# Macaron block (FFN, attention, FFN) on one core: another order of norm, unpacking and gelus at the head of both FFNs

## The reference, cut to what matters

```python
x = x + 0.5 * ffn(layernorm(x))            # "FFN 1"
x = x + attention(layernorm(x))            # 16 heads of 32, causal
x = x + 0.5 * ffn(layernorm(x))            # "FFN 2", the same weights

def layernorm(x, eps=1e-5):
    return (x - mean(x)) / sqrt(var(x) + eps)

def ffn(xt):                               # xt: 2048 x 512, MLP 4096
    gate = xt @ dequant(gate_W).T          # 4096 x 512
    up   = xt @ dequant(up_W).T            # 4096 x 512
    gelu = tanh(0.79788 * (gate + 0.044715 * gate**3)) * gate * 0.5 + gate * 0.5
    return (gelu * up) @ dequant(down_W).T # 512 x 4096
```

## Time and profile before

| | us |
|---|---|
| median of 3 runs | 3058.48 (3055.43 to 3061.62) |
| the profiled execution's own time | 3058.05 |
| its span (first to last instruction) | 3056.3 |
| PE busy in the span | 2944.6 (96%) |
| DVE, ACT, POOL busy | 1878.1, 1060.1, 758.6 |
| mean granted clock of PE, share of full speed | 0.982 |

### The profile page before, as it was taken

The page is one execution under the profiler, slowest core; times in us unless marked ns, Lnnn a source line. Parts: engine busy times, 40 slices in busy tenths (PEclk is TensorE's granted clock), DMA queues, the critical chain, the costliest instruction groups (busy, mean ns, idle before and its releaser), DMA issues. The chain is left out here.

```text
span 3056.3 us, 38836 instructions
## 1 busy us (share of the span) xinstructions
PE 2944.6 (96%) x13152; PEld 2208.8 (72%) x13152; DVE 1878.1 (61%) x3314; ACT 1060.1 (35%) x1797; POOL 758.6 (25%) x481
## 2 busy tenths in 40 slices
PE   5999999999999989999999999689999999999999
PEld 3788888888888858754454555368888888888887
DVE  7666565566565555566666665876556656556654
ACT  4322222222222222265565665243222222222222
POOL 4322222222222234400000002343222222222221
PEclk8999999999999989999999999799999999999999
DMA  3000000000000016822322331101000000000001
GB/s 96 21 28 22 27 27 21 21 27 24 24 27 21 1 45 130 220 54 52 62 55 52 62 78 64 45 14 33 23 21 27 21 27 27 21 21 27 21 14 55
DMA packets 120234, 126.75 MB, mean 41 GB/s; under 512 B 72728, under 2 KB 72984, under 8 KB 116820
## 3 DMA queue, kind: packets, MB, share of 16 engines
q1 hardware_dynamic: 120148, 125.71, 15.8%
HBM read 96.34 MB, written 29.34 MB: 41 GB/s over the span
## 5 line engine op out<-in xcount | busy, mean ns | idle before, releaser
L61 PE MATMUL psum<-ffn_x_high,ffn_w_high 128*128 128x512 f32 x2048 | 803.3, 392 | 18.6 <-DVE ffn_gelu L389 18.6
L62 PE MATMUL psum<-ffn_x_low,ffn_w_high 128*128 128x512 f32 x2048 | 799.2, 390 | 0.0
L63 PE MATMUL psum<-ffn_x_high,ffn_w_low 128*128 128x512 f32 x2048 | 798.9, 390 | 0.0
L526 POOL TENSOR_TENSOR ffn_inner<-ffn_gelu,ffn_inner 128x512 fp32r<-128x512 f32 x256 | 345.9, 1351 | 1156.8 <-ACT ffn_inner L471 1156.8
L379 DVE SCALAR_TENSOR_TENSOR ffn_gelu<-ffn_gelu,psum 128x512 f32<-128x512 f32 x256 | 175.9, 687 | 600.0 <-ACT ffn_gelu L464 599.9
L61 PEld LDWEIGHTS psum<-ffn_x_high,ffn_w_high 128*128 128x128 f32 x2048 | 386.1, 189 | 103.9 <-DVE ffn_gelu L389 21.9
L62 PEld LDWEIGHTS psum<-ffn_x_low,ffn_w_high 128*128 128x128 f32 x2048 | 385.9, 188 | 81.9 <-issue 2.0
L63 PEld LDWEIGHTS psum<-ffn_x_high,ffn_w_low 128*128 128x128 f32 x2048 | 385.8, 188 | 80.7
L61 PE MATMUL psum<-ffn_inner,ffn_w_high 128*128 128x512 f32 x1024 | 398.6, 389 | 0.2
L62 PE MATMUL psum<-ffn_inner,ffn_w_high 128*128 128x512 f32 x1024 | 398.4, 389 | 0.0
L63 PE MATMUL psum<-ffn_inner,ffn_w_low 128*128 128x512 f32 x1024 | 398.4, 389 | 0.0
(11 more groups left out here) (116 smaller groups left out, 3191.1 us busy)
## 6 DMA issues: line engine op xcount, KB each, us to landing
ffn_words<-packed SPq DMA_DIRECT2D x96, 256.0 KB
ffn_word_scales<-scales SPq DMA_DIRECT2D x96, 256.0 KB
qk_parts<-parts SPq DMA_DIRECT2D x32, 512.0 KB, 4.3
queries<-qk_parts SPq DMA_DIRECT2D x48, 256.0 KB, 4.1
keys<-qk_parts SPq DMA_DIRECT2D x48, 256.0 KB, 6.1
x<-x_in SPq DMA_DIRECT2D x4, 1024.0 KB, 14.5
v_parts<-parts SPq DMA_DIRECT2D x16, 256.0 KB, 4.7
values<-v_parts SPq DMA_DIRECT2D x16, 256.0 KB, 8.0
```

The source lines that it names most:

```text
L61: pe.matmul(out, w_high, x_high, start=first, stop=False, skip_group_check=True)
L62: pe.matmul(out, w_high, x_low, start=False, stop=False, skip_group_check=True)
L63: return pe.matmul(out, w_low, x_high, start=False, stop=last, skip_group_check=True)
L526: pool.tensor_tensor(inner[:, tb % 2, m, 1, :], product[m], f32(inner[:, tb % 2, m, 0, :]), ALU.subtract)\
```

## The change

`Norm.scale` is split in two: `invert` (the reciprocal) and `scale` (the four multiplications). In `ffn` the written order at the head changes on all four engines; in `project_in` each `scale` becomes `invert` and `scale` one behind the other, which is the order it had. No instruction is added or removed, and no buffer, wait or DMA is changed. GpSimd's `gelu_tiles` gets the argument `tiles` that DVE's and ACT's have, to take the tiles of a block one at a time.

```diff
--- before.py
+++ after.py
@@ -152,9 +152,11 @@
             act.wait_ge(self.normed_ready, KT * tb)
         act.activation(self.std[:], self.var_bank[tb % 2], ACT.Sqrt, bias=self.eps[:]).then_inc(self.std_ready, 1)
 
-    def scale(self, dve, tb):
+    def invert(self, dve, tb):
         dve.wait_ge(self.std_ready, tb + 1)
         dve.reciprocal(self.std[:], self.std[:]).then_inc(self.rstd_ready, 1)
+
+    def scale(self, dve, tb):
         dve.wait_ge(self.rstd_ready, tb + 1)
         for k in range(KT):
             tile = self.centred[tb % 2][:, k, :]
@@ -316,18 +318,22 @@
 
 
             n.mean(pe, 0)
-            n.mean(pe, 1)
-            n.variance(pe, 0)
+            if x_in is None:
+                n.mean(pe, 1)
+                n.variance(pe, 0)
+            else:
+                n.variance(pe, 0)
+                n.mean(pe, 1)
             n.mean(pe, 2)
+            gate_up_tile(0, 0, 0, 0, first=True, norm=True)
             n.variance(pe, 1)
-            gate_up_tile(0, 0, 0, 0, first=True, norm=True)
+            gate_up_tile(0, 0, 0, 1, first=True)
             n.mean(pe, 3)
-            gate_up_tile(0, 0, 0, 1, first=True)
+            gate_up_tile(0, 0, 1, 0, norm=True)
             n.variance(pe, 2)
-            gate_up_tile(0, 0, 1, 0, norm=True)
             gate_up_tile(0, 0, 1, 1)
+            n.variance(pe, 3)
             gate_up_tile(0, 0, 2, 0, norm=True)
-            n.variance(pe, 3)
             gate_up_tile(0, 0, 2, 1)
             down(0, 0, 0)
             down(0, 0, 1)
@@ -411,26 +417,29 @@
             dve.memset(eps[:], EPS).then_inc(n.constants_ready, 1)
 
             n.sum_pairs(dve, 0)
+            n.centre(dve, 0)
             unpack(0, 0, GATE, first=True)
-            n.centre(dve, 0)
+            n.sum_square_pairs(dve, 0)
             unpack(0, 0, UP, first=True)
-            n.sum_square_pairs(dve, 0)
+            n.invert(dve, 0)
+            n.scale(dve, 0)
             n.centre(dve, 1)
-            n.scale(dve, 0)
             n.sum_square_pairs(dve, 1)
+            n.centre(dve, 2)
+            n.invert(dve, 1)
+            gelu_tiles(0, 0, 0, [0], first=True)
+            n.scale(dve, 1)
+            n.sum_square_pairs(dve, 2)
+            gelu_tiles(0, 0, 0, [1], first=True)
+            n.centre(dve, 3)
             unpack(0, 0, DOWN)
-            n.scale(dve, 1)
-            n.centre(dve, 2)
-            n.sum_square_pairs(dve, 2)
-            gelu_tiles(0, 0, 0, first=True)
-            n.centre(dve, 3)
+            n.invert(dve, 2)
             n.scale(dve, 2)
-            gelu_tiles(0, 0, 1, [0])
             n.sum_square_pairs(dve, 3)
-            gelu_tiles(0, 0, 1, [1])
-
+            gelu_tiles(0, 0, 1)
             dve.wait_ge(n.std_ready, NTB)
             dve.memset(signal[:], 0.0).then_inc(down_free, KT)
+            n.invert(dve, 3)
             n.scale(dve, 3)
             add_down(0, 0, 0)
             gelu_tiles(0, 0, 2)
@@ -481,20 +490,21 @@
 
 
             act.wait_ge(n.constants_ready, 2)
+            n.square(act, 0)
             weight_high(0, 0, GATE)
-            n.square(act, 0)
+            n.standard_deviation(act, 0)
             weight_high(0, 0, UP)
-            n.standard_deviation(act, 0)
+            n.high(act, 0)
             n.square(act, 1)
-            n.high(act, 0)
             n.standard_deviation(act, 1)
-            weight_high(0, 0, DOWN)
+            n.square(act, 2)
+            gelu_tiles(0, 0, 0, [0])
             n.high(act, 1)
-            n.square(act, 2)
-            gelu_tiles(0, 0, 0)
+            gelu_tiles(0, 0, 0, [1])
             n.standard_deviation(act, 2)
             n.square(act, 3)
             n.high(act, 2)
+            weight_high(0, 0, DOWN)
             gelu_tiles(0, 0, 1)
             n.standard_deviation(act, 3)
             n.high(act, 3)
@@ -520,8 +530,8 @@
                 pool.tensor_tensor(w_low[s][:, :, piece, :], weight[:, q % 2, :, :],
                                    f32(w_high[s][:, :, piece, :]), ALU.subtract).then_inc(w_low_ready, 1)
 
-            def gelu_tiles(gg, s, tb):
-                for m in range(2):
+            def gelu_tiles(gg, s, tb, tiles=range(2)):
+                for m in tiles:
                     pool.wait_ge(inner_high_ready, 16 * gg + (8 * s + 2 * tb + m + 1))
                     pool.tensor_tensor(inner[:, tb % 2, m, 1, :], product[m],
                                        f32(inner[:, tb % 2, m, 0, :]), ALU.subtract)\
@@ -543,10 +553,11 @@
             weight_low(0, 0, UP)
             n.low(pool, 0)
             n.sum_pairs(pool, 3)
+            gelu_tiles(0, 0, 0, [0])
             n.low(pool, 1)
-            gelu_tiles(0, 0, 0)
+            gelu_tiles(0, 0, 0, [1])
+            n.low(pool, 2)
             weight_low(0, 0, DOWN)
-            n.low(pool, 2)
             gelu_tiles(0, 0, 1)
             n.low(pool, 3)
             gelu_tiles(0, 0, 2)
```

## The result

| | before | after |
|---|---|---|
| median, us (8 runs each) | 3057.48 (3053.5 to 3061.62) | 3048.19 (3046.57 to 3051.95) |
| profiled execution: time, span | 3058.05, 3056.3 | 3048.34, 3046.5 |
| mean granted clock of PE | 0.982 | 0.985 |

The ratio after to before is 0.9972 (95% interval 0.9963 to 0.998), so the change gives 0.28%, 9.3 us by the medians and 9.8 by the two spans. I had said 11.6.

A forecast was written before the change was run, and what follows sets the result against it. PE was taken to bound the kernel, with gains only at the two FFN heads. FFN 1's 3.2 us and FFN 2's 8.4 made 11.6 off 3058.05, so 3046.4 for the profiled execution and 3047 for the median; range 3040 to 3054.

The forecast's parts named there:

- What bounds it: Whole kernel: PE is busy 96% of the span, so time can be won only at the FFNs' two heads, where PE waits.
- Part 1: Start of FFN 2: the first block's multiplications start at 1971.4 instead of 1976.90, 5.5 us earlier.
- S: Start of the first block's four multiplications in an FFN's head; 31.24 and 1976.90 us in the kernel before.
- Part 2: Start of FFN 1: the first block's multiplications start at 29.8 or 32.0, taken as 30.9, 0.3 us earlier.
- The table load: ACT in FFN 1, between centre and squares: 1.28 us, nearly all hidden by GATE; the skill's price was about 2.66 us.
- Part 3: Both heads, from S to the end of tile (2,1): 59.1 us instead of 62.0, 2.9 us less per FFN.
- The sum: Both FFNs: FFN 1 gains 3.2 us and FFN 2 8.4, together 11.6.
- my middle: FFN 1: 30.9 us for S, taken between 29.8 and 32.0, with 1.1 us kept to both sides.
- The reading of the stretched steps: DVE instructions with SBUF operands alone that meet a POOL instruction wait it out, then they take turns.
- Rival D: Heads: PE's clock stays low before tile (2,0), costing 11.7 us per FFN, time 3070; chance 0.05.
- one of my signs of being wrong: Heads: the forecast would be wrong if PE's clock is at half in tiles (0,1) to (1,1).
- Rival B: Heads: more DVE steps meet POOL work, gain only 5.9 us, time 3052.6; chance 0.2 shared with another rival.

The follow-up runs named there:

- e12: Changed kernel plus one one-column ScalarE instruction at the start of each FFN, loading its table early; ratio to the kernel before 0.9973.
- e7: Changed kernel with third sum of squares ahead of the second block's multiplications and third variance ahead of tile (1,0); ratio to the kernel before 0.9967.
- e4: Changed kernel with GpSimd making the second block's low parts ahead of the first gelu tile's low part; ratio to the kernel before 0.9956, median 3044.8 us.
- e5: Changed kernel with 14 matmuls without use in PE's idle gap ahead of tile (1,0); ratio to the kernel before 0.9971.
- e9: Changed kernel with the edits of e4 and e7 together; ratio to the kernel before 0.9954, median 3043.3 us.
- e10: e9 plus matmuls without use ahead of and inside tile (0,0) and ahead of the fourth variance; ratio to the kernel before 0.9968, median 3048.05 us.
- e11: e9 with GpSimd adding the third block's pairs behind UP's low part in FFN 1 alone; ratio to the kernel before 0.9953.
- e3: Only the first block's norm moved ahead, the rest ordered as in the kernel before, from the second block's sum of squares on; ratio to that kernel 0.9986.

## Why the prediction was right, and what was mis-sized

- **What bounds it.** Right: all of the gain lies in the two heads, 9.72 of 9.8 us, and PE streams behind them as before.
- **Part 1.** S in FFN 2: 5.5 us earlier said, 5.54 measured. Two steps of UP waited one GpSimd instruction each (2.71 and 2.71), as priced.
- **Part 2.** S is 29.8 or 32.0, said the prediction; the profiles show 29.5 and 31.8. Right, and so was the reason: the third meeting hangs on whether the third block's pairs, free when PE ends the second mean, start ahead of UP's last steps. PE ended that mean at 25.3 in the changed kernel (25.1 said). But the changed kernel's profile shows the lucky case and seven of eleven the late one. The table load was hidden (e12), and a longer price for it was not seen.
- **Part 3** is the term that was mis-sized: S to the end is 60.89 and 60.47, not 59.1, so the new order gave 1.0 and 1.4 us there instead of 2.9. Three stretches make it up.
  - S to second reciprocal: 14.73 and 14.06, said 13.8. In FFN 1 the low part of UP ran into the first block's multiplications (4.64 for 3.57), which the sum had at nothing; tile (0,0) ended at S + 12.1 and 11.4 (said 11.2).
  - Second to third reciprocal: 22.66 and 22.83, said 21.0. This is the larger miss, and the step that failed is the third root, which hangs on tile (1,0). The tile ended at S + 34.7 and 34.2 (said 32), and the reciprocal waited 1.5 and 1.6 us (said 0.4). e7 takes the root off the tile, and the wait is gone. Part of the lateness is the low part of the first gelu, which I had let run beside the second block's multiplications unpriced: they took 4.63 instead of 3.5, the low parts ended 0.5 later behind the second reciprocal than said, and e4, which moves it, wins 0.8 and 0.3 of this stretch. The larger part is the clock, by an estimate from the rows: from the last low part (59.39) to the end of the tile (64.26) PE needed 4.9 us, where the last 15 matmuls at 0.226 are 3.4. No run separates the two, as e5 did not keep the clock up.
  - Third reciprocal to end: 23.50 and 23.58, where the prediction's times make 24.3. Here it went 0.7 to 0.8 better than said. PE's idling ahead of the fourth variance was 4.49 in both (said 4.5).
- **The sum.** FFN 1: 2.75 for 3.2, where an S 1.4 earlier than my middle made up for most of the 1.9 lost behind it; that is luck, and with S late the same order takes 91.05 to 92.45 us there, not 90.40. FFN 2: 6.97 for 8.4, all of it part 3.
- **The reading of the stretched steps** held: who starts first keeps the other waiting to its end. The Trainium skill says the same ("SBUF — State Buffer", section SBUF: two separate sides: the shared pair of ports is locked for the whole instruction by whoever starts first), and by that rule the gelu's low part, starting first, had to be in the sum; the trace agrees, with 4.63 against 3.56 us.
- **Rival D**, the clock, was half right in mechanism, and one of my signs of being wrong did come: the clock at half in tiles (0,1) to (1,1). It falls in tile (1,0), but rises again within it, and what it delays is a root, whose wait is 1.5 us a head; 11.7 never came up. The Trainium skill's case of small idle spells that make the clock swing ("TensorE: Matmul & The Clock Gate", section A second HAM failure mode: psum-queue depth-cycling) is thus seen in one tile here. Rival B's path, meetings with GpSimd, took a part of what was missing as well, in part 3 though, not in UP.
- **Part of the difference is not the change's.** The stretch between the heads was 1855.2 us in both of the profiles compared here, but 1851.6 to 1857.5 in others of this study, so that the median came within 1.2 us of the 3047 forecast is partly chance.

## What to carry to other kernels

When instruction lists of several engines are reordered by hand, price each moved instruction against what the engine that shares its path to memory does at that moment; one such meeting moved S by 2 us here, where the whole change gave FFN 1 2.75. A dependent matmul step (here a variance) belongs into a gap that PE has anyway, ahead of the tile that would otherwise stand before it. And when a start can fall on either side of a meeting, quote both values and take several profiles before crediting one.

## What the runs showed of the hardware that was not expected

PE entered tile (1,0) of FFN 1 at the full clock in e5, and the clock still fell to 0.50 within the tile, where it got three matmuls at a time and the longest single wait was 1.24 us. In e9, FFN 1, where the same tile's waits were 1.04, 0.66, 0.28 and 0.27 us, it stayed at 1.00. But in FFN 2 of e9 it fell to 0.50 behind waits of 1.04 and 0.65, and the profiles of e10 and e11 repeat both outcomes. I had reckoned with long gaps alone. The waits in the tile do not decide it by themselves, and what does is not shown.

And the same order lands in two distinct places in FFN 1, some 2 us apart, by a difference of a few tenths between DVE and GpSimd: UP's last step began at 25.18 in both e4 and e3, GpSimd's third pairs began at 25.36 in the one, just behind its start, and at 24.96 in the other, just ahead of it.
